# Thirty-two gathered products ahead of the count pipeline, and two small DMAs cut into fourteen

## The reference

```
h  = gcn_conv(h, W1, b1);  h = h / norm(h)          # pass 0: sum of source rows by destination
ev = sigmoid([h[src], h[dst]] @ We1 + be1)
na = relu(segment_sum(ev * h[src], dst) @ Wn1 + bn1)   # pass 1
ev2 = sigmoid([na[src], na[dst]] @ We2 + be2)
g  = relu(segment_sum(ev2 * na[src], dst) @ Wn1 + bn1) # pass 2
out = gcn_conv(g, weights ev2, W2, b2)                 # pass 3
```

## Time and profile before

| what | us |
|---|---|
| median of 3 runs | 3349.76 (3348.71 to 3354.33) |
| the profiled execution | 3348.71 |
| its span in the trace | 3346.9 |
| PE busy | 2635.7 (79%) |
| DVE busy | 2111.6 (63%) |
| ACT busy | 1617.9 (48%) |
| POOL busy | 1866.2 (56%) |

### The profile page before, as it was taken

One profiled execution on the slowest core, in us unless ns is written; L12 is line 12 of the kernel. 1 busy time (PEld: TensorE's weight loads), 2 busy tenths in 40 slices (PEclk: granted clock), 3 DMA queues, 4 the chain that ended last, 5 costly groups with the idle time before them and its releaser, 6 DMA issues.

```text
span 3346.9 us, 58780 instructions
## 1 busy us (share of the span) xinstructions
PE 2635.7 (79%) x16470; PEld 2291.0 (68%) x16470; DVE 2111.6 (63%) x6199; ACT 1617.9 (48%) x3249; POOL 1866.2 (56%) x1816
## 2 busy tenths in 40 slices
PE   0667667898997677777789899999999676777775
PEld 0344446888885667666678788888888566666665
DVE  5567676665635566666675567666676456666667
ACT  7256565666666454554454444444444422233232
POOL 5345456555405666667720666666661267776673
PEclk9788898999999898988899899999999888888998
DMA  4244445555542333333322444444442433333333
GB/s 114 80 147 152 147 155 192 193 208 211 189 174 78 100 100 106 107 98 114 99 71 79 124 134 135 135 135 135 134 134 81 141 98 97 107 106 100 112 99 94
DMA packets 185594, 419.58 MB, mean 125 GB/s; under 512 B 36655, under 2 KB 136700, under 8 KB 175533
## 3 DMA queue, kind: packets, MB, share of 16 engines
q10 hardware_dynamic: 83703, 244.23, 20.6%
q0 software_dynamic: 61472, 140.49, 15.3%
q1 hardware_dynamic: 40118, 31.23, 3.0%
HBM read 311.35 MB, written 102.16 MB: 124 GB/s over the span
## 4 chain that ended last, share of the span: by engine, by line
PE 67%; issue 13%; DVE 9%; ACT 3%; ACTq 3%; another core or an unknown queue 2%; DMA 1%; DVEq 1%; POOL 1%; SPq 0%; POOLq 0%
PE ps L1117 18%; PE ps_high L1109 16%; PE ps_high L1117 12%; PE ps L1057 7%; PE ps_high L1075 3%; PE ps L1041 3%; ACT tab_area L769 2%; PE ps_high L1070 2%; ACTq L377 1%; PE ps_high L1196 1%; DVE acc L1592 1%; DVE tab_area L1521 1%; PE ps L1229 1%; DVE weights L1568 1%
## 5 line engine op out<-in xcount | busy, mean ns | idle before, releaser
L601 POOL DMA_INDIRECT rows<-table,edge_src x1664 | 1759.9, 1058 | 1164.0 <-SPq L496 604.0
L1109 PE MATMUL ps_high<-rows,weights 128*128 x2784 | 648.0, 342 | 385.2 <-issue 235.6
L1117 PE MATMUL ps<-tab_area,acc 128*128 128x129 f32 (+2 forms) x4410 | 824.2, 327 | 7.4 <-issue 6.1
L1109 PEld LDWEIGHTS ps_high<-rows,weights 128*128 128x128 f32 x2784 | 473.6, 204 | 486.9 <-issue 292.9
L1117 PEld LDWEIGHTS ps<-tab_area,acc 128*128 128x128 f32 x4410 | 698.6, 206 | 52.3 <-issue 7.2
L863 ACT ACTIVATE step<-xbuf,rows 128x128 f32 x928 | 358.0, 394 | 690.4 <-PE ps_high L1109 312.8
L1592 DVE TENSOR_TENSOR acc<-acc 128x640 f32<-128x640 f32 x735 | 604.9, 823 | 102.3 <-ACT acc L872 64.7
L1117 PE MATMUL ps_high<-tab_area,acc 128*128 128x129 f32 (+2 forms) x2940 | 588.3, 326 | 0.3 <-issue 0.3
L1575 DVE TENSOR_TENSOR acc<-acc,ps_high 128x129 f32 (+1 forms) x948 | 335.1, 354 | 384.9 <-PE ps_high L1109 187.8
L769 ACT ACTIVATE tab_area<-ps_high x816 | 404.4, 496 | 304.9 <-PE ps_high L1075 178.7
L1117 PEld LDWEIGHTS ps_high<-tab_area,acc 128*128 128x128 f32 x2940 | 478.0, 206 | 29.8 <-issue 1.2
(11 more groups left out here) (242 smaller groups left out, 2177.8 us busy)
## 6 DMA issues: line engine op xcount, KB each, us to landing
acc<-counts ACTq DMA_DIRECT2D x105, 1120.0 KB
counts<-tab_area ACTq DMA_DIRECT2D x51, 1568.0 KB
acc<-counts ACTq DMA_DIRECT2D x25, 1568.0 KB
rows<-table,edge_src POOLq DMA_INDIRECT x1664
table<-tab_area SPq DMA_DIRECT2D x6, 903.0 KB, 4.8
table<-acc SPq DMA_DIRECT2D x7, 448.0 KB, 4.2
table<-tab_area SPq DMA_DIRECT2D x6, 455.0 KB, 3.9
table<-tab_area SPq DMA_DIRECT2D x6, 448.0 KB, 3.0
```

Of the source, the lines that this page charges most:

```text
L601: nc.gpsimd.indirect_dma_start(rows[:, t % UNROLL, 0:row_floats[k]], None, tables[k], bass.IndirectOffsetOnAxis(ap=edge_src[:, t:t + 1], a ...
L1109: nc.tensor.matmul(ps[DENSE_BANKS + m % PAIR_BANKS][:, 0:WIDTH[k]], weights[:, m % W_RING, :], rows[:, bass.ds(known["slots"][m % UNROLL], ...
L1117: ins = nc.tensor.matmul(ps[j][:, 0:WIDTH[k]], gate_blocks[:, n % S_RING, j * PART:(j + 1) * PART], table[:, h, 0:WIDTH[k]], start=(h == 0 ...
```

## The change

```diff
-PAIRS_FROM, PAIRS_EARLY = 2 * FLUSH, 176
+PAIRS_FIRST, PAIRS_EARLY = 32, 176
...
 def pairs_at(s):
     early = SURE * FLUSH
     if s <= early:
-        return max(s - PAIRS_FROM, 0) * PAIRS_EARLY // (early - PAIRS_FROM)
+        return PAIRS_FIRST + s * (PAIRS_EARLY - PAIRS_FIRST) // early
...
                 for part, to in enumerate((cell_to, zero_to)):
-                    sp.dma_start(to, slot_row(part).rearrange("c (i u) -> c i u", u=2 * QUAD)).then_inc(ld_slot_rows, 16)
+                    for c in range(SLOT_COLS):
+                        sp.dma_start(to[:, c, :, :], slot_row(part)[c:c + 1, :].rearrange("c (i u) -> c i u", u=2 * QUAD)).then_inc(ld_slot_rows, 16)
...
-            act.wait_ge(ld_slot_rows, 16 * 6)
+            act.wait_ge(ld_slot_rows, 16 * (2 * SLOT_COLS + 4))
...
-                pe.wait_ge(slot_rows_ready, 1)
+                for m in range(pairs_at(0)):
+                    multiply(m)
                 for r in range(REGIONS):
                     last = nc.tensor.matmul(ps_high[:, r * REGION:(r + 1) * REGION], no_cells[:, 0:PART], no_cells[:, :],
                                             start=True, stop=True, skip_group_check=True)
                 last.then_inc(cells_cleared, 1)
-                pe.wait_ge(ld_slot_rows, 16 * 6)
+                pe.wait_ge(ld_slot_rows, 16 * (2 * SLOT_COLS + 4))
...
                 weigh(0)
+                for m in range(pairs_at(0)):
+                    add_pair(m)
                 for b in range(LM_RING - 1):
                     mark(b)
```

## The result

The changed kernel took 3394.48 us (median of 4, 3388.78 to 3397.36) where the kernel before took 3349.24 on the same chip: a ratio of 1.0131, 95% interval 1.0112 to 1.0148. That is +45 us. The forecast was slower by 28 us, 3377.5 us, with a range up to 3392: the sign came out, and the place (32 pairs ahead of ACT's first copy), the size did not.

A forecast was written before the change was run, and what follows sets the result against it. ACT's copies with their turns to PE and register loads were taken to pace the early stage, PE the late one. +35.2 − 4.1 − 2.7 = +28.4 us gave 3377.5 us, range 3364 to 3392 for 8 in 10.

The forecast's parts named there:

- part 2: Start of the first edge pass: 32 pairs ahead of the clears move ACT's first copy by +35.2 us, bounds 31 to 42.
- first term: Start of the first edge pass: ACT's first copy moves from 143.31 to 178.5 us, +35.2 us.
- ACT's start given back: ACT's first 16 slots: of 8.2 us slow start, by late code or cold restart, the middle returns, −4.1 us.
- steps to the 26th DMA: Early slots: 144 pairs instead of 176 beside them and one register read fewer, −2.7 us, bounds 0 to 4.8.
- from there to the end of the pass: From slot 416 on: same schedule in both kernels, PE passes the late start on undiminished, 0 us.
- SP's split at nothing: SP queue before the first relay: 14 DMAs take 9.4 us more, hidden by the gathers; 3 us without that cover.
- The gathers set the pace: Prologue: 32 pairs need tiles up to 30, issued at 167.8 us, landed 4.5 us later; clears end at 176.3.
- Between 1.2 us and 3.6 us for four: Prologue's last quad, pairs 28 to 31 on PE and DVE over two banks: 2.0 us taken.
- From the clears to the first copy: PE to ACT: five clears 2.0 us, then two table reads of 1.02 us each, first copy at 178.5 us.
- No moved pair saved 1.1 us: First rival, slots 32 to 416: pairs pace the early stage, 32 fewer save 59 us, total 3322 us; chance 0.04.
- the shift did not vanish late in the pass: Second rival, late first pass: slack absorbs the shift, 3350 to 3355 us; chance 0.06 together with the fourth.
- third rival: SP queue: issues cost 2 us each, first relay at 168 us, 19.4 us later than the sum, 3397 us; chance 0.06.

The follow-up runs named there:

- base: Kernel before with each of the four values from memory that a semaphore waits against passed through a bitwise and with 1023; 3181.10 us, ratio 0.9988.
- Held gathers: Base with POOL's first-pass gathers held until ACT's 16th copy, on the chip where the kernel before took 3327.4 us; 3337.28 us, ratio 1.0028.
- first prompt pair: Changed kernel with the base's bitwise and, beside the base; 3208.85 us, ratio 1.0079, +27.8 us over the base; the second pair gave 3203.60 us, +22.1 us.

## Why the prediction was wrong, step by step

The step that failed is part 2's, "Now PE must work through 32 pairs", in its size: +35.2 us for ACT's first copy, with an upper bound of 42. It measured +58.0, because the handovers between SP, PE and DVE were late there, which the sum had at nothing beyond 3 us of late relays. The sum of the steps, from POOL's first gather on (us; "prompt" is the mean of the two pairs of base and changed kernel):

| | forecast | first chip | prompt semaphores |
|---|---|---|---|
| first gather to clears, changed kernel | 44.5 | 62.8 | 42.9 |
| first gather to first copy, changed kernel | 48.7 | 71.0 | 47.8 |
| the same, kernel before or base | 13.5 | 13.5 | 11.4 |
| **first term** | **+35.2** | **+57.5** | **+36.4** |
| ACT's start given back | −4.1 | −8.6 | −0.4 |
| steps to the 26th DMA | −2.7 | −6.6 | −6.2 |
| from there to the end of the pass | 0 | −2.1 | −5.4 |
| sum | +28.4 | +40.2 | +24.4 |
| the whole, profiled executions | | +33.8 | +31.6 and +6.1 |
| median against median | +28 | +45.2 | +27.8 and +22.1 |

Behind the end of the pass the kernels are the same, yet the pairs of traces differ there by −6.9 us on the first chip and by +3.2 and −11.5 us on the prompt ones. A single pair of traces tells the terms inside the pass; it doesn't tell the whole to better than some 10 us. With prompt semaphores the total near the forecast is partly luck: nearly nothing was given back at ACT's start, and the steps and the end of the pass gave back more than forecast.

- **SP's split at nothing: right.** 14 issues of 0.63 us, and no share in the prologue (47.6 us without it, 47.8 with it). The cover named for it, the gathers, was there; with prompt semaphores POOL is idle 0.30 us before tile 16, in the first trace 4.4 us. The Trainium skill (DMA: Bandwidth & Descriptors, Anatomy of one DMA) fits its fixed cost near 2 us to DMAs issued from GpSimd, and lays most of it on completion; on SP's queue one issue follows the other after 0.63 us here, so the fixed cost isn't time of the issue.
- **The gathers set the pace: right where semaphores are prompt,** 42.9 us to the clears for 44.5. The landing took 2.7 us there (tile 30 issued at 167.29, its quad begun at 169.97), not 4.5: the 4.5 was read off a relay on SP's queue whose neighbours took 0.7 us each, so that row held late semaphores already. On the first chip the step failed by 18.3 us to the clears. Against the prompt traces it is 19.9 us: tile 16 came 4.1 us later (24.2 us after the first gather for 20.1), and 15.8 us more were lost in the pairs. "Between 1.2 us and 3.6 us for four" was taken from rows in which 176 adds waited 1.9 us for an unknown queue, and used for 32 adds that waited 15.1.
- **From the clears to the first copy: 4.2 us forecast,** 4.9 with prompt semaphores, 8.2 on the first chip. ACT's first register read stands 5.8 us behind the start of the clears there, and 2.4 where semaphores are prompt. With the 18.3 us it makes up the 22.3 us that the first term is over.
- **Slips of the sum.** 176.3 + 2.04 is 178.3, not 178.5, and the terms named for the lower bound of 31 give about 33. Neither bears on the outcome.
- **ACT's start.** I left it between code that arrives late and a cold restart, and took half. It was neither: late semaphores beside the sixteen gathers. Held gathers take it away on a chip that has it, and on a prompt chip it doesn't exist. In the changed kernel the first copy comes 27.8 us after POOL's 32nd gather, and all of it was given back, though five more gathers ran beside these 16 copies, 1.2 to 3.3 us apart. So gathers beside the start aren't enough by themselves; in the kernel before, the end of a dense run of sixteen fell there.
- **The steps** gave back 6 us, 0.2 us a pair, above the 0 to 4.8 that I allowed. The last row, −2 to −5 us between the 26th DMA and the end of the pass, I had excluded; in the first prompt pair about half of it falls between the 28th and the 31st DMA, in the second none does, and its cause stays open.
- **The rivals.** No moved pair saved 1.1 us, the shift did not vanish late in the pass, and the issues didn't take 2 us. The third rival's 3397 us lies near the measured 3394 by luck: its mechanism is absent. The overrun of 17 us between the medians came from something that none of them named.

The row that warned was on the table: the earlier trace rows has "remote", a wait on an unknown queue, in a program that runs on one core. I read it as an accident of ACT's start and priced it as something that could only be given back. The kernel before has these waits all over its first trace,

```profile
ACT acc L872 <- remote: 152.4, 45, 13.3
ACT step L863 <- remote: 91.0, 29, 9.9
DVE tab_area L1575 <- remote: 87.4, 28, 12.9
DVE acc L1575 <- remote: 83.0, 26, 9.4
```

(waits: us in total, times, longest), 138 of them with 433 us in all; the base's trace on a prompt chip has none. A chain of 32 pairs through PE and DVE, placed beside the longest run of gathers in the pass, has some 64 handovers on the path (two for each pair). That is where such waits had to be dear, and a bound for it could have been had from the earlier trace rows: 4.5 us for one.

What isn't shown: why the first chip and the one of 3327 us have late semaphores and the five others don't (each was used on one occasion, so it may be the occasion), and whether these waits are the whole of the 165 us between 3349 and 3184 us. No kernel here beats the kernel before: the best, the base with prompt semaphores, is the same within its interval.

## What to carry to other kernels

Work moved ahead of a pipeline's start costs its own critical path, here 32 gathers and some 36 us, and is paid back only by what it cost in its old place, here 0.2 us a pair in the steps; ask for that second number first, and if it is below the first, don't move. Price a chain that goes back and forth between engines by its handovers too, and look in the waits for releasers that can't exist in the program: here they stood where handovers were late. Time a few per cent on more than one chip before explaining its size.

## What the runs showed of the hardware

- The same kernel took 3349 and 3327 us on two chips and 3180 to 3193 on five others. The traces of the first two have 119 to 154 waits on an unknown queue (340 to 449 us), those of the five others none.
- On the first two, while and after gathers are issued 1.25 us apart, some semaphore instructions of SP take about 0.7 or 1.4 us in place of 0.017. In the trace with the held gathers, where SP's relays before it were prompt, the first such one starts 7.4 us after the first gather.
- A register load of 16 32-bit neighbours takes 1.00 to 1.04 us on ACT, of 16 16-bit numbers 3.36 to 3.43, side by side or not. A bounds test of a loaded value takes 147 + 18 ns, and 928 of them on ACT, with those of SP and PE, made the kernel 174 us longer in one execution; a bitwise and in their place made no difference (0.9988).
